# A transformer block with self and cross attention on one core: the logits of two heads placed on the two row halves of the PE array

## The reference

```python
c_proj = silu(c) @ W_mod + b_mod              # shift, scale and gate, for attention and for the MLP
x = x + gate_a * (softmax(q k^T / 4) v @ W_proj + b_proj)          # 16 heads of 16 features, from modulate(_ln(x))
x = x + softmax(q_c k_c^T / 4) v_c @ W_cproj + b_cproj             # q_c from _ln(x), k_c and v_c from _ln(context)
x = x + gate_m * (gelu(modulate(_ln(x)) @ W_mlp1 + b_mlp1) @ W_mlp2 + b_mlp2)
```

## Time and profile before

| | |
|---|---|
| median of 3 runs | 1815.16 us |
| the profiled execution: its time, its span | 1817.13 us, 1815.3 us |
| first `maxima` matmul | 55.2 us into the span |
| mean granted TensorE clock (1 is 2.4 GHz) | 0.96 |
| matmuls, VectorE, ScalarE and GpSimd instructions | 14066, 2765, 2151, 975 |

### The profile page before, as it was taken

The page is one execution under the profiler, slowest core; times in us unless marked ns, Lnnn a source line. Parts: engine busy times, 40 slices in busy tenths (PEclk is TensorE's granted clock), DMA queues, the critical chain, the costliest instruction groups (busy, mean ns, idle before and its releaser), DMA issues.

```text
span 1815.3 us, 44393 instructions
## 1 busy us (share of the span) xinstructions
PE 1576.2 (87%) x14066; PEld 1053.4 (58%) x14066; DVE 1293.0 (71%) x2765; ACT 1062.8 (59%) x2151; POOL 722.3 (40%) x975
## 2 busy tenths in 40 slices
PE   3668799998999899998989899899999999989875
PEld 1334466665666666665656666566666666665543
DVE  4567677777777777777777777777777777775531
ACT  3234566666666566666656666666666666666441
POOL 3322344443334444443344444333444444333422
PEclk8688999999999999999999999999999999999887
DMA  4123222223333232223322223333323232332101
GB/s 147 51 70 71 75 73 79 76 80 77 90 90 83 65 81 70 78 82 84 90 76 73 77 72 80 76 90 87 82 70 80 71 81 78 84 84 66 43 25 30
DMA packets 187591, 137.93 MB, mean 76 GB/s; under 512 B 42849, under 2 KB 178178, under 8 KB 187426
## 3 DMA queue, kind: packets, MB, share of 16 engines
q1 hardware_dynamic: 187426, 135.47, 27.7%
HBM read 56.60 MB, written 9.57 MB: 36 GB/s over the span
## 4 chain that ended last, share of the span: by engine, by line
PE 57%; DVE 19%; issue 11%; POOL 4%; SPq 4%; DMA 4%; ACT 1%; POOLq 0%; DVEq 0%; ACTq 0%
PE dense_ps L373 11%; PE dense_ps L374 10%; PE dense_ps L375 10%; PE o_ps L697 9%; PE max_ps L667 8%; PE exp_ps L681 6%; DVE mx_cross L1003 4%; DVE mx_self L1003 2%; DVE ot_self L1027 2%; PE dense_ps L611 2%; SPq L495 2%; DVE ot_self L1025 2%; DVE stats L950 1%; POOL xn L1125 1%; POOL rs L1119 1%
## 5 line engine op out<-in xcount | busy, mean ns | idle before, releaser
L816 ACT ACTIVATE probs<-exp_ps 128x512 f32<-128x512 f32 x1024 | 585.7, 599 | 355.7 <-PE exp_ps L681 344.4
L1003 DVE TENSOR_REDUCE mx_cross<-max_ps 128x2 f32<-128x512 f32 x512 | 337.6, 681 | 126.3 <-PE max_ps L667 124.6
L1003 DVE TENSOR_REDUCE mx_self<-max_ps 128x2 f32<-128x512 f32 x512 | 343.3, 681 | 88.5 <-PE max_ps L667 84.8
L667 PE MATMUL max_ps<-k_stack_self,q_stack_self 96*128 96x256 f16 x1024 | 202.0, 280 | 39.6 <-issue 22.5
L681 PE MATMUL exp_ps<-q_stack_cross,k_stack_cross 128*128 128x512 f16 x512 | 196.5, 386 | 7.1 <-ACT probs L816 4.4
L667 PE MATMUL max_ps<-k_stack_cross,q_stack_cross 96*128 96x256 f16 x1024 | 198.7, 277 | 2.1 <-DVE mx_cross L1003 1.6
L681 PE MATMUL exp_ps<-q_stack_self,k_stack_self 128*128 128x512 f16 x512 | 197.4, 387 | 3.5 <-ACT probs L816 2.4
L1116 POOL TENSOR_SCALAR ve<-mv 128x2 f32<-128x2 f32 x96 | 18.5, 193 | 436.7 <-DVE mv L956 436.7
L1163 POOL TENSOR_TENSOR g_split<-G,g_split 128x512 f16<-128x512 f32 x128 | 162.8, 1299 | 22.2 <-DVE g_split L1049 22.2
L667 PEld LDWEIGHTS max_ps<-k_stack_self,q_stack_self 96*128 96x128 f16 x1024 | 86.1, 98 | 120.0 <-DVE mx_self L1003 61.4
L373 PE MATMUL dense_ps<-mlp_hi,g_split 128*128 128x256 f16 x512 | 140.4, 274 | 3.5 <-POOL g_split L1163 3.5
(11 more groups left out here) (216 smaller groups left out, 3458.5 us busy)
## 6 DMA issues: line engine op xcount, KB each, us to landing
q_stack_self<-split_q SPq DMA_DIRECT2D x192, 64.0 KB, 2.6
k_stack_self<-split_k SPq DMA_DIRECT2D x96, 128.0 KB, 3.3
q_stack_cross<-split_qc SPq DMA_DIRECT2D x192, 64.0 KB, 2.6
k_stack_cross<-split_kc SPq DMA_DIRECT2D x96, 128.0 KB, 3.5
X<-in_x SPq DMA_DIRECT2D x32, 256.0 KB, 2.8
rows_a<-rows_a_dram SPq DMA_DIRECT2D x32, 256.0 KB, 3.9
o_n_self<-o_sb_self SPq DMA_DIRECT2D x64, 128.0 KB, 3.1
Ctx<-in_ctx SPq DMA_DIRECT2D x32, 256.0 KB, 2.8
```

What stands on the lines that cost most here:

```text
L667: mm = pe.matmul(max_ps[:, t % 2, ab * T:(ab + 1) * T], q_stack[kind][0:96, b.u, p, ab * T + qt * P:ab * T + (qt + 1) * P], k_stack[kind][ ...
L816: nc.scalar.activation(probs[:, t % 8], exp_ps[:, t % 2], ACT.Exp).then_inc(exp_taken[kind], 1)
L1003: nc.vector.tensor_reduce(mx[kind][:, t % 2, :, t // 2], max_ps[:, t % 2].rearrange("p (a k) -> p a k", a=2), AX_X, ALU.max).then_inc(max_ ...
```

## The change

- The two heads of a pair go to partitions 0 to 49 and 64 to 113 of both stacks, in their own columns 0 to 255. There are no zero blocks, and `q_stack` is half as wide. A head has 3 x 16 rows for the parts (`PART` = 48) and two for the maximum.
- `maxima` and `exps` are called for two tiles at once, in even slots only. Each call has four matmuls of 256 columns over 48 (50) rows, at `tile_position` (0, 0) and (64, 0) in turn. The first head's results go to tile 0 and the second's to tile 1. A call waits until both tiles of the call before have been read.
- VectorE and ScalarE take the two tiles one after the other in the same even slot.
- `k` and `kc` are stacked by six transfers instead of three. The two fills of `q_stack` with zeros are gone, and `b_mod_rows` moves to `probs`.
- `values` reads its four heads from four tiles of `probs` instead of two pairs, and waits for the copy of the group before instead of the one before that.
- `EXP_START` and `AV_AFTER` are 6, and most places in `PLAN` and some in `BANK` are new.

```diff
-EXP_START = 5
-AV_AFTER = 5
+EXP_START = 6
+AV_AFTER = 6
...
-        return None if b is None else (kind, b, s)
+        return None if b is None or s % 2 else (kind, b, s)
...
-        return None if b is None else (kind, b, (s - EXP_START) % TILES)
+        return None if b is None or (s - EXP_START) % 2 else (kind, b, (s - EXP_START) % TILES)
...
-        q_stack = {k: sb(f"q_stack_{k}", [P, 2, PAIRS, 2 * T], F16) for k in KINDS}
+        q_stack = {k: sb(f"q_stack_{k}", [P, 2, PAIRS, T], F16) for k in KINDS}
...
-        STACK_DMAS = {"q": 6, "k": 3, "qc": 6, "kc": 3}
+        STACK_DMAS = {"q": 6, "k": 6, "qc": 6, "kc": 6}
+        PART = 3 * HD
...
+                    stack_of = (q_stack if n[0] == "q" else k_stack)[kind]
                     for part in parts:
-                        if n[0] == "k":
-                            nc.sync.dma_start(k_stack[kind][32 * part:32 * part + 32, b.u], split[n][:, sign]
+                        for ab in range(2):
+                            at = 64 * ab + HD * part
+                            nc.sync.dma_start(stack_of[at:at + HD, b.u], split[n][64 * ab:64 * ab + 64, sign]
...
-                if t >= 2:
-                    pe.wait_ge(max_taken[kind], b.n * TILES + t - 1)
-                elif (prev := previous(it, max_order, MAX_LAG, kind)):
-                    pe.wait_ge(max_taken[prev[0]], prev[1].n * TILES + TILES - 1 + t)
-                for ab in range(2):
-                    mm = pe.matmul(max_ps[:, t % 2, ab * T:(ab + 1) * T],
-                                   q_stack[kind][0:96, b.u, p, ab * T + qt * P:ab * T + (qt + 1) * P],
-                                   k_stack[kind][0:96, b.u, p], start=True, stop=True)
-                mm.then_inc(max_ready[kind], 1)
+                    if (prev := previous(it, max_order, MAX_LAG, kind)):
+                        pe.wait_ge(max_taken[prev[0]], prev[1].n * TILES + TILES)
+                else:
+                    pe.wait_ge(max_taken[kind], b.n * TILES + t)
+                for qt in range(2):
+                    for ab in range(2):
+                        rows = slice(64 * ab, 64 * ab + PART)
+                        mm = pe.matmul(max_ps[:, ab, qt * T:(qt + 1) * T], q_stack[kind][rows, b.u, p, qt * P:(qt + 1) * P],
+                                       k_stack[kind][rows, b.u, p], start=True, stop=True, tile_position=(64 * ab, 0))
+                        if qt == 1:
+                            mm.then_inc(max_ready[kind], 1)
...
+                for kt in range(2):
+                    for ab in range(2):
+                        rows = slice(64 * ab, 64 * ab + PART + 2)
+                        mm = pe.matmul(exp_ps[:, ab, kt * T:(kt + 1) * T], k_stack[kind][rows, b.u, p, kt * P:(kt + 1) * P],
+                                       q_stack[kind][rows, b.u, p], start=True, stop=True, tile_position=(64 * ab, 0))
+                        if kt == 1:
+                            mm.then_inc(exp_ready[kind], 1)
...
-                if g >= 2:
-                    pe.wait_ge(o_copied[kind], b.n * 4 + g - 1)
+                if g >= 1:
+                    pe.wait_ge(o_copied[kind], b.n * 4 + g)
...
+                        for ab in range(2):
+                            dve.wait_ge(max_ready[kind], b.n * TILES + t + ab + 1)
+                            nc.vector.tensor_reduce(mx[kind][:, :, ab, t // 2],
+                                                    max_ps[:, ab].rearrange("p (q k) -> p q k", q=2), AX_X, ALU.max
+                                                    ).then_inc(max_taken[kind], 1)
```

More of the change, by code:

```diff
@@ L35 @@
 PLAN = {
[L37 to L43, removed]
@@ L51 @@
[L51 to L55, removed]
[6 rows of a table removed]
-    "y": (4, 1, 13), "y_add": (4, 1, 13), "store": (4, 1, 15),
-}
-BANK = {"m_self": 1, "m_cross": 2, "qc": 2, "cproj": 0, "tc": 1, "kc": 2, "t3": 0, "mlp1_0": 1, "mlp1_1": 2,
-        "mlp1_2": 0, "mlp1_3": 1, "vc": 2, "t1": 1, "proj": 0, "mlp2": 2, "q": 1, "k": 0, "v": 1, "t2": 0}
+    "load_x": (-1, 0, 7), "cols_a": (-1, 0, 8), "ln1": (-1, 0, 14), "norm1": (-1, 0, 11), "t1": (-1, 1, 3),
@@ new lines @@
+    "t1_hi": (-1, 1, 2), "t1_lo": (-1, 1, 4), "q": (-1, 1, 6), "q_hi": (-1, 1, 7), "q_lo": (-1, 1, 7),
+    "stack_q": (-1, 1, 4), "k": (-1, 1, 9), "k_hi": (-1, 1, 8), "k_lo": (-1, 1, 11), "stack_k": (-1, 1, 12),
+    "v": (-1, 1, 9), "v_hi": (-1, 1, 10), "split_self": (0, 1, 0), "m_self": (0, 1, 1), "m_copy_self": (0, 1, 2),
+    "o_gather_self": (1, 0, 10), "o_recip_self": (1, 0, 10), "r_out_self": (1, 0, 10), "r_back_self": (1, 1, 0),
+    "o_norm_self": (1, 1, 2), "o_hi_self": (1, 1, 3), "rows_a": (1, 0, 5), "xr": (0, 1, 14), "proj": (1, 1, 4),
@@ new lines @@
+    "x2": (1, 1, 5), "ln2": (1, 1, 6), "norm2": (1, 1, 7), "t2": (1, 1, 14), "t2_hi": (1, 1, 14),
+    "t2_lo": (2, 0, 1), "qc": (2, 0, 3), "qc_hi": (2, 0, 2), "qc_lo": (2, 0, 4), "stack_qc": (2, 0, 6),
+    "xc": (3, 0, 2), "load_c": (1, 1, 4), "lnc": (1, 1, 9), "normc": (1, 1, 4), "tc": (1, 1, 13),
+    "tc_hi": (1, 1, 12), "tc_lo": (1, 1, 14), "kc": (2, 0, 7), "kc_hi": (2, 0, 6), "kc_lo": (2, 0, 9),
+    "stack_kc": (2, 0, 14), "vc": (2, 0, 15), "vc_hi": (2, 1, 0), "split_cross": (3, 0, 0), "m_cross": (3, 0, 0),
@@ L69 @@
+    "m_copy_cross": (3, 0, 2), "o_gather_cross": (3, 1, 5), "o_recip_cross": (3, 1, 11), "r_out_cross": (3, 1, 6),
+    "r_back_cross": (3, 1, 15), "o_norm_cross": (3, 1, 9), "o_hi_cross": (4, 0, 2), "cproj": (4, 0, 5),
[6 rows of a table added]
+}
+BANK = {
+    "m_self": 1, "m_cross": 2, "qc": 1, "cproj": 0, "tc": 1, "kc": 2, "t3": 2, "mlp1_0": 1, "mlp1_1": 2,
+    "mlp1_2": 0, "mlp1_3": 1, "vc": 0, "t1": 1, "proj": 0, "mlp2": 2, "q": 1, "k": 0, "v": 1, "t2": 0,
+}
 DENSE = {n: BANK[n] for n in sorted(BANK, key=lambda n: PLAN["mlp2_0" if n == "mlp2" else n][1:])}
@@ L656, in maxima @@
             def maxima(it, kind, b, t):
-                p, qt = t // 2, t % 2
+                p = t // 2
                 if t == 0:
@@ L672, in exps @@
             def exps(it, kind, b, t):
-                p, kt = t // 2, t % 2
+                p = t // 2
                 if t == 0:
                     pe.wait_ge(mrow_in[kind][b.u], dmas(b, 2))
-                if t >= 2:
-                    pe.wait_ge(exp_taken[kind], b.n * TILES + t - 1)
-                elif (prev := previous(it, exp_order, EXP_LAG, kind)):
-                    pe.wait_ge(exp_taken[prev[0]], prev[1].n * TILES + TILES - 1 + t)
-                pe.matmul(exp_ps[:, t % 2], k_stack[kind][:, b.u, p, kt * P:(kt + 1) * P], q_stack[kind][:, b.u, p],
-                          start=True, stop=True).then_inc(exp_ready[kind], 1)
+                    if (prev := previous(it, exp_order, EXP_LAG, kind)):
+                        pe.wait_ge(exp_taken[prev[0]], prev[1].n * TILES + TILES)
+                else:
+                    pe.wait_ge(exp_taken[kind], b.n * TILES + t)
@@ L1094, in _ @@
             nc.gpsimd.memset(neg_half[:], -0.5)
-            nc.gpsimd.memset(q_stack["self"][:], 0.0).then_inc(zeroed, 1)
             nc.gpsimd.memset(k_stack["self"][:], SHIFT_UNIT).then_inc(zeroed, 1)
@@ L1108, in last_setup @@
                 pool.wait_ge(sp_set, 16 * 6)
-                nc.gpsimd.memset(k_stack["cross"][:], SHIFT_UNIT)
-                nc.gpsimd.memset(q_stack["cross"][:], 0.0).then_inc(consts, 1)
+                nc.gpsimd.memset(k_stack["cross"][:], SHIFT_UNIT).then_inc(consts, 1)
             def normalise(b, k, src):
```

45 lines of the change are left out of this document (16 added, 29 removed), and 12 rows, old and new, of the table PLAN.

## The result

The changed kernel takes 1754.91 us (median of 4 runs, 1749.29 to 1761.07). Before it, on the same chip, the old kernel took 1816.5 us. The ratio is 0.9661, with a 95% interval of 0.9622 to 0.9700: faster by 3.4%, 61.6 us. I had forecast 1725 us and a range of 1630 to 1805. The direction and the range held, and the gain was a third smaller than forecast.

What follows compares the result with a forecast made beforehand. TensorE set the old period; after the change TensorE and VectorE are level. Double slots 46.9 + loop's top 1.0 + transfers 0.2 + clock 0.4 = 48.5 us instead of 51.7, over 28 periods 90 us less: 1725 us, range 1630 to 1805.

Steps and rivals of the forecast that it cites:

- the overlap: Logits matmuls on two array halves run fully side by side: 0.22 us a call instead of 0.44, 7.0 us of TensorE gained.
- The rival without overlap: Halves do not overlap or weights wait: TensorE keeps 14.0 us for logits, period 53.3 us, about 1860 us; chance 0.12.
- the changes of shape: TensorE's switches between matmul tile shapes: 38 instead of 20 per period, 0.09 us each, 1.6 us more.
- 12 us behind: In the old kernel TensorE, with 45.8 of 51.7 us, sets the period, and VectorE was put 12 us behind it.
- the transfers: Six more SyncE transfers a period, with `stack_k` issued behind `r_out_cross`: 0.2 us on the period, bounds 0 and 1.5.
- the loop's top: TensorE's wait at the start of the loop: 1.0 us per period, added to the double slots' 46.9 us.
- fill and drain: Stages before and after the steady part, 313 us: no change taken, bounds 15 us either way.
- VectorE sets 15.3: Half 0, slots 0 to 13: VectorE is the longer engine with 15.3 us, against 12.6 for TensorE.
- the clock: Lower TensorE clock expected in slots 2 and 3 of half 1: 0.4 us on the period, bounds 0 and 1.7.
- The rival of a clock that falls twice in every batch: TensorE's clock drops twice in every batch: period 50.5 us, about 1780 us; chance 0.15.
- small things: Moved steps such as `rows_b` and `xm`, the `q_stack` fills and the `values` wait: no time added to the period.
- if a transfer is waited for in every batch: One of three signs that would make the prediction wrong, beside calls costing 0.4 us and a dropping clock.

Runs made afterwards that it cites:

- twice: The changed kernel with each call of `maxima` and `exps` issuing its four matmuls twice into the same banks: 1819.78 us, ratio 1.0027.
- k_hi_on_scalar: The changed kernel with the four transfers of `k`'s high part issued on ScalarE's queue instead of SyncE's: 1726.33 us, ratio 0.9509.
- half_reduce: The changed kernel with VectorE's maximum reductions over only 128 of the 256 keys: 1734.72 us, ratio 0.9559.

## Why the prediction was right, and where it was off

**Right: the overlap.** A call costs 0.22 to 0.23 us, as forecast, and `twice` shows that the gain hangs on it. The rival without overlap had 1860 us, and the same TensorE time measured 1820. It was dearer on paper because I had put all of TensorE's time on the path, where a quarter of what was added showed. For the weight loads I had weighed the Trainium skill's rule ("TensorE: Matmul & The Clock Gate", Part 3, The mechanism), that a load overlaps a running matmul only in another row group. The calls of this trace don't bear out the 0.2 us that it would add: four loads and four matmuls fit into 0.23 us.

**Right: the changes of shape.** 0.09 to 0.10 us each, 36 a batch against my 38. By these prices TensorE's work is the 40.4 us of the forecast at the full clock; its busy time, 1167.02 / 27 = 43.2 us, also holds the way through the array and the lower clock. VectorE's 39.4 was measured as 1073.00 / 27 = 39.7. That VectorE is "12 us behind" TensorE was misread: 12 us is its distance from the old period, and 6.4 that from TensorE's 45.8 us of work.

**Mis-sized: the transfers.** The step "I put 0.2 us on the period (bounds 0 and 1.5)" measured 2.1 us, beyond the bound. I had let `stack_k` start with `r_out_cross` and take 6.5 us to landing, against 6.2 us of work for TensorE and 2.1 more in every second batch. In the 27 batches it is 7.8 us on average from the issue of `r_out_cross` to the first `maxima` (0.5 for that issue, 4.3 for the six, 3.0 from there to the matmul), and TensorE runs out of work after 5.6. I had also found that the later `stack_kc` and `stack_q` do no harm, each by itself. What I had not done is lay all issues of half 1 one behind another: 24 of them fill 17 us of the queue almost without a gap, from `q`'s stack over the gathers and `r_out_cross` to `k_stack`, the last to be ready and the first to be needed. That the stack costs time and not only a wait is shown by `k_hi_on_scalar`: 28 us, of it 20 in the steady part. The rest of the 2.1 us only covered the loop's top (1.0 us in the forecast, 34.2 / 27 = 1.3 us in that run).

The steady part missed by 49.44 - 48.5 = 0.94 us a period, 25 us, of which the stack's 20 us are the part that a run shows. With the 5 us in fill and drain (forecast 0, bounds 15), and 3 us because 28 periods had been counted and 27 lie between batches 4 and 31, that is about the 34 us between the forecast for the profiled execution (1727) and its time (1761).

**Right in sum, wrong in place: "VectorE sets 15.3".** The double slots by the longer engine gave 22.5 us for the first half and 24.4 for the second, and the loop's top and the stack, 1.2 us, lie between the second half and the next batch: 25.6. Measured between the first `maxima` of each kind, the first half takes 24.2 us (slots 0 to 13 16.7 against 15.3, slots 14 and 15 7.5 against 7.2) and the second 25.2, with 2.1 us for the stack and 0.3 at the loop's top in it. So the first half is 1.7 us too long and the second a little shorter than forecast, although the wait that I had mis-sized lies in it. Nor is VectorE alone the limit where I had put it: `half_reduce` took 8.3 us out of its period, and slots 0 to 13 gained 1.2 us where the forecast's own sums give 2.7. TensorE's waits for the stack, `ot_self`, `xn` and `ot_cross` stayed or grew instead. Why the first half is too long is open; the lower clock, which lies almost wholly in it, is one candidate.

**Right in amount, wrong in place: the clock.** I had forecast one stretch of the lower clock a batch, 3.4 us long, in slots 2 and 3 of half 1, and priced it at 0.4 us. There are 22 stretches in 27 batches, 3.0 us a period, elsewhere. The rival of a clock that falls twice in every batch, with 3.4 us of delay from some 7 us at the lower level, did not come true. I cannot say what these 3.0 us cost: between 0, if all lies behind the other engines, and 1.5 (half of 3.0). The comparison of first halves gives 0.8 us a period there (24.2 - 23.5, before rounding), and does not show that the period keeps it.

**Under-rated: the places.** I treated the moves as small things around a change of the matmuls. Logits alone cost 6 to 11%, places alone 1.5%, and both together save 3.4%. My cost sheet had the logits' 5.4 us as gain and the places as corrections to it. The runs show that neither gains anything by itself.

**What was forecast as evidence.** Pairs a few ns apart: yes. VectorE's waits down from 6.4: to 4.8. TensorE's waits for the reductions up: from 0.2 to 1.8 us a period. Clock of 0.95 or more: 0.97. No wait for `k_stack` over 0.5 us: no, and this was the one that I had named as what would make the prediction wrong, "if a transfer is waited for in every batch". It was in 24 of 27.

Left open are the price of the low clock, why the first half is longer than forecast, and what the loop's top waits for. I did not try a stack in fewer transfers.

## What to carry to other kernels

When steps are moved, write out each transfer queue as a row of issues with their durations, and follow the one that is needed first through it. A cost for each transfer by itself misses the queue, and here four issues on another queue were worth half as much as the whole change (28 of 62 us). An engine's work is worth only what shows in the time. Here 7.0 us of added TensorE work showed as 1.76, and 8.3 us of removed VectorE work as 1.0; adding or leaving out work and timing it shows this, and the busy share does not. A new form of an operation and the schedule around it should be judged together, for each alone may lose.

## What the hardware showed that I had not expected

- Matmuls of 48 rows in the two row halves ran side by side in whatever order they were issued. With the two of one half first, a call still took 0.23 us, and the third matmul started 0.1 us before the second in all 1024 calls.
- A small transfer (64 KB into 16 partitions) holds its queue for 3.84 / 6 = 0.64 us, and one queue with 24 issues in 17 us becomes what TensorE waits for.
- At the top of the loop TensorE stands up to 3.5 us with no releaser in the trace (34.2 us at 12 places in `k_hi_on_scalar`, every second batch). In the changed kernel only 7.2 us of it are left, since the wait for the stack covers it.
